# Value products one pair later, padded new values and reordered loads in a paged attention kernel on one core

## The chip, the core and the metric

The kernel runs on one core of a Trainium2 chip. The metric is device time in microseconds (us) from one launch, all of it, constants and layouts of the host excluded. Engines are called as the profile calls them: PE is the matrix engine (PEld its weight loads), DVE the vector engine, ACT the scalar engine, POOL the general-purpose engine, SP the one that here only issues DMAs (SPq, ACTq: issues by SP and ACT).

## The reference

Two residual layers on `x`, shape (32, 32, 512), float32. The first is grouped-query attention (32 query heads, 8 key heads, 128 wide) with a paged cache: each batch row has 16 pages of 32 keys, named by its row of a block table, and 32 new keys and values of its own.

```python
q = _rope(_rmsnorm(x @ Wq.T, q_norm_w), pos)           # 32 heads
k = _rope(_rmsnorm(x @ Wk.T, k_norm_w), pos)           # 8 heads
v = x @ Wv.T
k_all = concat([k_cache[block_table], k], axis=1)      # 512 cached + 32 new keys per row
v_all = concat([v_cache[block_table], v], axis=1)
scores = q @ k_all.T * SCALE                            # cached keys past cache_seqlens masked
o = softmax(scores) @ v_all
x = x + o @ Wo.T
x = x + (x @ W.T + 2 * lora(x, top-2 gates))           # second layer
```

## The kernel before

The 1024 rows of x are eight **tiles** of 128 rows; a tile is four batch rows (`ROWS`) of 32 positions. The eight key heads are four **groups** of two (`GK`). The main loop runs groups outside and tiles inside, 32 **steps** `i = g * TILES + t`. Within a step the work is eight **pairs** `p` (batch row `p // 2`, key head `p % 2`); a pair has 128 query rows (4 query heads of the group by 32 positions) against 544 keys. Every engine has its own instruction list, written by hand in a function `body(g, t, final)`; they meet only at semaphores, and each engine runs its list strictly in order. Steps t = 1 to 5 are one loop body, the others are written out.

Products that need more than one pass split both factors in a rounded half (`_hi`) and a rest (`_lo`), and multiply three times (`three_pass`, L193). Per pair:

- PE `score` (L193, to SX), three passes over 17 key slots; the scores of pair p + 2 are made while pair p is worked on.
- DVE `minimum` (L992) adds the mask and finds the extreme value; ACT `exponent` (L776); DVE `normalise` (L997, L999).
- PE `turn_probs` (L537, L538) transposes the probabilities to PT in five matmuls; ACT `take_pT` (L772) copies them to pT; PE `weigh` (L550, L554) multiplies them with the values into O, transposed: four full products with cached values `v_rows` (each two instructions in the trace) and one with the new values `v_new`. The new values of the four batch rows lie in one tile, 32 partitions each, so this last product uses 32 of the array's 128 rows: `v_new[rows, cols]` against `pT[rows, L:L + P]`.
- DVE `take_o` (L1008, L1010) splits O into oT_hi and oT_lo.

In the PE list, pair p is `turn_probs(p)`, `score(p + 2)`, some projections of the next step, `weigh(p)`. After the last pair come the 24 products of `project_out` (to MISC), which DVE adds to y (`add_y`, L1027). The add of L1027 ends a step in the tables below.

In the same step the next step's q, k, v are projected (`proj`, to PROJ, three blocks of 12 products), taken by ACT (`take_block`), squared by ACT, and rotated: DVE `rotate` (L975, L979), then POOL `make_rstd` (L1258, L1261) and `rotate_sum` (L1269, L1278); PE `turn_k` and `turn_q` transpose the result.

POOL also issues the gathers of cached values (`gather`, L1225, four indirect DMAs for each batch row), makes the rotation table (`make_table`), and copies the new values (`keep_v`, L1286). SP fetches the keys: 12 pages of each batch row, 48 a step (L267), ACT the other 4; the page's byte offset is read from the list `pages` into a register (`read_pages`). SP also loads x, the mask, weights (`next_half`), the running y, and the cached keys of the next group, which PE, ACT and DVE turn and split in eight **units** (`turn_unit`) and SP stores back to DRAM as `kT_pages` (`store_unit`). Before a group's first step all eight stores must have landed (`ku_stored`); ACT and SP wait for this in step t = 7.

## Time and profile before

| | |
|---|---|
| median of 3 runs | 1611.72 us (1608.89 to 1619.95) |
| the profiled execution, its own time | 1600.16 us |
| its span, first to last instruction | 1598.3 us |
| PE busy | 1379.9 us, 86% |
| POOL busy | 948.5 us, 59% |
| DVE busy, ACT busy | 823.5 us, 662.0 us |
| mean granted clock of PE | 0.923 |
| HBM traffic | 188 GB/s over the span |

The busy time of an engine leaves out register reads, semaphores and the issue of DMAs by SP and ACT, so SP has none at all and must be read from its timeline. PE's busy time counts the modelled end of a matmul, which overlaps the next one's start. Step ends, by the end of L1027's adds, are at 139.0 (step 0), 354.3 (step 5), 510.7 (step 8), 1521.5 (step 30) and 1551.7 us (step 31). Steps with t = 6, 7 and 0, around the change of a group, also carry the weight loads; they are called boundary steps below (nine of them between step 6 and step 24), and the other 21 of steps 1 to 30 plain steps.

### The profile page before, as it was taken

Reading aid. Unit: us, or ns where it says so; the run is one execution under the profiler, and the core shown is the slowest. Engines: PE = TensorE matmul, PEld = TensorE weight load, DVE = VectorE, ACT = ScalarE, POOL = GpSimd, SP = SyncE. Lnnn points to the kernel's source line nnn. Section 1 sums busy time; section 2 is a strip of 40 time slices with the busy share of each in tenths; the row PEclk is TensorE's granted clock in tenths of the full one; section 3 lists DMA queues with packets and bytes.
Section 4 is the critical chain, followed back from the end, with each engine's and each line's share of the span. In section 5 each row is a group of like instructions: output and inputs, shape, how many; then the busy total and the mean of one; then the engine's idle time right before and its main releaser. Section 6 shows DMA issues by size and latency. Waiting matters only on the chain.

```text
span 1598.3 us, 33745 instructions
## 1 busy us (share of the span) xinstructions
PE 1379.9 (86%) x8000; PEld 1171.2 (73%) x8000; DVE 823.5 (52%) x2193; ACT 662.0 (41%) x1742; POOL 948.5 (59%) x1270
## 2 busy tenths in 40 slices
PE   4369999998788999999887999999878989888899
PEld 3258787777676777778676787877767877777777
DVE  5445455455455445555545555545545454545544
ACT  3243444444343344444344444444434344434431
POOL 4446666665565667666555666666655666666500
PEclk9588999898999899999898999999879899989999
DMA  8675766678656676677667666667666565656721
GB/s 293 194 211 156 202 193 199 187 202 246 181 177 182 174 201 190 189 200 212 195 178 212 191 199 197 187 191 222 203 197 183 149 182 165 176 168 174 211 77 53
DMA packets 393726, 299.69 MB, mean 187 GB/s; under 512 B 45905, under 2 KB 349297, under 8 KB 393458
## 3 DMA queue, kind: packets, MB, share of 16 engines
q1 hardware_dynamic: 292386, 193.37, 41.3%
q0 software_dynamic: 24576, 67.14, 14.5%
q10 hardware_dynamic: 76656, 37.98, 8.3%
q8 instruction: 38, 0.62, 0.2%
q14 instruction: 70, 0.57, 0.1%
HBM read 271.27 MB, written 29.13 MB: 188 GB/s over the span
## 4 chain that ended last, share of the span: by engine, by line
PE 42%; issue 16%; SPq 15%; DVE 9%; ACT 4%; DMA 4%; another core or an unknown queue 4%; ACTq 3%; POOL 1%; DVEq 0%; POOLq 0%
PE MISC L193 11%; PE O L550 8%; SPq L267 8%; PE SX L193 6%; PE PROJ L193 5%; PE O L554 4%; PE PT L537 4%; DVE soft L992 2%; ACTq L267 2%; ACT pT L772 2%; DMA stage<-in_wqkv 2%; SPq L319 2%; DVE rope_v L979 2%; SPq L266 1%
## 5 line engine op out<-in xcount | busy, mean ns | idle before, releaser
L1225 POOL DMA_INDIRECT v_rows<-in_kv,step_idx x512 | 506.6, 990 | 195.6 <-issue 132.8
L550 PE MATMUL O<-pT,v_rows 128*128 128x128 f32 x2048 | 304.3, 295 | 132.1 <-ACT pT L772 124.6
L776 ACT ACTIVATE soft<-soft,min_all 128x544 f32<-128x544 f32 x256 | 191.7, 749 | 524.0 <-DVE min_all L992 373.3
L550 PEld LDWEIGHTS O<-pT,v_rows 128*128 128x128 f32 x2048 | 276.2, 205 | 173.8 <-ACT pT L772 154.6
L1008 DVE CAST oT_hi<-O 128x128 fp32r<-128x128 f32 x256 | 73.8, 288 | 409.1 <-PE O L554 303.8
L772 ACT ACTIVATE pT<-PT 128x640 f32<-128x640 f32 x256 | 179.7, 702 | 177.6 <-PE PT L538 103.8
L193 PE MATMUL SX<-kT,qT_hi 128*128 128x288 f32 (+1 forms) x1024 | 242.5, 327 | 8.0 <-DVE qT_lo L1021 3.9
L992 DVE CUSTOM_DVE_ANT_0 soft<-SX,mask 128x544 f32<-128x544 f32 x256 | 184.4, 720 | 52.2 <-PE SX L193 23.8
L193 PEld LDWEIGHTS SX<-kT,qT_hi 128*128 128x128 f32 x1024 | 170.7, 202 | 17.8 <-issue 6.7
L537 PE MATMUL PT<-ident,soft 128*128 128x128 f32 x1024 | 180.7, 303 | 2.1 <-issue 2.1
L999 DVE TENSOR_SCALAR soft<-soft,rden 128x544 f32<-128x544 f32 x256 | 157.4, 615 | 9.1
L193 PE MATMUL PROJ<-w_hi,x_hi 128*128 128x512 f32 x384 | 152.5, 397 | 7.8 <-ACT raw L739 4.8
L1269 POOL TENSOR_TENSOR rope_u<-rope_u,rope_v 128x512 f32<-128x512 f32 (+1 forms) x96 | 109.2, 1138 | 80.6 <-DVE rope_v L979 80.6
L193 PE MATMUL SX<-kT,qT_lo 128*128 128x288 f32 (+1 forms) x512 | 155.1, 303 | 0.0
L193 PE MATMUL PROJ<-w_hi,x_lo 128*128 128x512 f32 x384 | 151.9, 396 | 0.0
L193 PE MATMUL PROJ<-w_lo,x_hi 128*128 128x512 f32 x384 | 151.7, 395 | 0.0
L537 PEld LDWEIGHTS PT<-ident,soft 128*128 128x128 f32 x1024 | 123.3, 152 | 32.2 <-issue 6.6
L554 PE MATMUL O<-pT,v_new 32*128 32x128 f32 x512 | 132.2, 340 | 0.0
L1258 POOL TENSOR_SCALAR meansq<-sumsq 128x4 f32<-128x4 f32 (+1 forms) x96 | 23.1, 240 | 158.9 <-ACT squares L746 128.6
L193 PE MATMUL MISC<-wo_hi,oT_hi 128*128 128x512 f32 x256 | 113.0, 441 | 3.7 <-DVE oT_lo L1010 3.6
L193 PE MATMUL MISC<-wo_lo,oT_hi 128*128 128x512 f32 x256 | 105.1, 411 | 0.0
L554 PEld LDWEIGHTS O<-pT,v_new 32*128 32x128 f32 x512 | 80.4, 196 | 33.5 <-issue 5.8
(205 smaller groups left out, 2170.0 us busy)
## 6 DMA issues: line engine op xcount, KB each, us to landing
kT<-kT_pages SPq DMA_DIRECT2D x1536, 64.0 KB
kT<-kT_pages ACTq DMA_DIRECT2D x512, 64.0 KB
mask<-mask_rows SPq DMA_DIRECT2D x64, 272.0 KB
kT_pages<-k_split SPq DMA_DIRECT2D x24, 512.0 KB
stage<-in_wqkv SPq DMA_DIRECT2D x22, 512.0 KB
x_raw<-in_xT SPq DMA_DIRECT2D x32, 256.0 KB
stage<-in_wo SPq DMA_DIRECT2D x16, 512.0 KB
v_rows<-in_kv,step_idx POOLq DMA_INDIRECT x512
```

What stands on the lines that cost most here:

```text
L193: mm = nc.tensor.matmul(out_ps, a, b, start=(c == 0 and k == 0), stop=(c == stop_at and k == 2))
L267: eng.dma_start(kT[:, b, j, :, :, :].rearrange("p z h s -> p (z h s)").bitcast(U8), kT_bytes[bass.ds(at, PAGE_BYTES)].rearrange("(d n) -> ...
L537: nc.tensor.transpose(PT[:, c * P:(c + 1) * P], probs[:, p % 2, c * P:(c + 1) * P], ident[:, :])
L550: nc.tensor.matmul(O[:, 0:P], v_rows[:, b, c, h * D:(h + 1) * D], pT[:, c * P:(c + 1) * P], start=c == 0, stop=False)
L554: nc.tensor.matmul(O[:, 0:P], v_new[rows, cols], pT[rows, L:L + P], start=False, stop=True).then_inc(sm["pv_done"], 1)
L772: nc.scalar.activation(pT[:, :], PT[:, 0:L + P], ACT.Copy).then_inc(sm["pT_ready"], 1)
L776: nc.scalar.activation(probs[:, p % 2, 0:KEYS], scores[:, p % 2, :], ACT.Exp, bias=min_all[:, p:p + 1], scale=-1.0, accum_out=den[:, p:p + ...
L992: V.tensor_tensor_reduce(scores[:, p % 2, :], SX[:, SX_AT[p % 2]:SX_AT[p % 2] + KEYS], mask[:, b, :], 1.0, BIG, ALU.add, ALU.min, min_all[ ...
L999: V.tensor_scalar(probs[:, p % 2, 0:KEYS], probs[:, p % 2, 0:KEYS], rden[:, p:p + 1], None, ALU.mult).then_inc(sm["probs_ready"], 1)
L1008: V.tensor_copy(hi, src).then_inc(sm["o_hi_ready"], 1)
L1225: G.indirect_dma_start(v_rows[:, b, c, :], None, v_half[:, :], bass.IndirectOffsetOnAxis(ap=step_idx[:, b * LC + c:b * LC + c + 1], axis=0 ...
L1269: G.tensor_tensor(rope_u[:, 0:w], rope_u[:, 0:w], rope_v[:, 0:w], ALU.add).then_inc(sm["sum_ready"], 1)
```

## The change

1. **PE order.** `weigh(p)` moves behind `turn_probs(p + 1)` and `score(p + 3)` of the following pair; pT gets two buffers. Over a step's end `turn_probs` of the next step's pair 0 and `score` of its pair 2 go ahead of `project_out`, which is split in three parts with `weigh` of pair 7 after the first. ACT and DVE lists follow.
2. **New values.** POOL writes, in place of the copy `v_new` (128 x 256), the tile `v_own` (128 x 4 x 256): for each of the four batch rows all 128 partitions, zero outside its own 32. The last product of `weigh` then uses all 128 rows.
3. **Order of loads.** A key unit is turned at pair 6 of the step before it is due (unit u in step u - 1; unit 0 at pair 2 of step 0), where it was at pair 1 of step u - 1 and pairs 2 and 3 of step 0. The weight halves move in HI_AT and LO_AT, and SP issues them at other places; half 5 is now the first load after the unit's store in t = 7. SP waits for the stored y after two batch rows of pages, not before the first. POOL makes the table of step i + 2 near the end of step i, where it made the table of i + 1 at the start.
4. **Page lists.** The byte offsets of all 32 steps are made at the start, four groups at once, and stored in DRAM (`page_bytes`); a step loads its own 64 (`load_list`), and registers are read at fixed addresses.
5. **Start.** SP issues the first key loads ahead of x and the weights, PE turns all eight units first, the split units are staged in wo_hi and wo_lo, ACT no longer waits for the page stores before block 2, and the halves that POOL split are split by DVE.
6. To make room: q_rot shares rope_v's memory (DVE's `rotate` then waits for `q_turned`), `squares` has two slots, the sign of the sine moves from a table into DVE's `scalar_tensor_tensor`, and the key turn goes to PROJ.

The core of the diff:

```diff
-        squares = sb("squares", [P, 512], BF16)
+        squares = sb("squares", [P, 2, D], BF16)
         sumsq = sb("sumsq", [P, NBLK, REP])
         meansq = sb("meansq", [P, REP])
         rstd = sb("rstd", [P, REP])
-        q_rot = sb("q_rot", [P, 512])
+        q_rot = rope_v
         k_rot = sb("k_rot", [P, GK * D])
         v_next = sb("v_next", [P, GK * D])
-        v_new = sb("v_new", [P, GK * D])
+        v_own = sb("v_own", [P, ROWS, GK * D])
...
+        HI_AT = ((6, 1), (6, 2), (6, 4), (6, 6), (7, 0), (7, 2), (0, 0), (0, 1), (0, 4), (0, 5))
+        LO_AT = ((6, 2), (6, 3), (6, 5), (6, 7), (7, 1), (7, 3), (0, 1), (0, 2), (0, 5), (0, 6))
+        L1_HI_AT = ((6, 1), (6, 2), (6, 5), (6, 6))
+        L1_LO_AT = ((6, 2), (6, 3), (6, 6), (6, 7))
         WO_FIRST = 2 * NBLK
...
-            if t == 0:
-                return {2: 0, 3: 1}.get(p)
-            return t + 1 if t < TILES - 1 and p == 1 else None
+                return t + 1 if p == 6 else None
+            if t == 0 and p == 2:
+                return 0
+            return t + 1 if t < TILES - 1 and p == 6 else None
 
         def next_tile(g, t):
...
+            def load_list(i):
+
+                sp.dma_start(pages[:, :], page_dram[bass.ds(i, 1), :]).then_inc(sm["pages_in"], 16)
+
...
-                    next_half(g + 1, 0)
-                    next_half(g + 1, 1)
-                if final and fixed and t == TILES - 2:
-                    for m in range(2):
-                        sp.wait_ge(sm["w_lo_ready"], GROUPS * HALVES + m - 1)
-                        sp.dma_start(stage[:, m, :, :], w1T.rearrange("p (c n) -> p c n", c=KC)[:, 2 * m:2 * m + 2, :]
-                                     ).then_inc(sm["stage1_in" if m else "stage0_in"], 16)
+                if not final:
+                    if fixed and t == 0:
+                        load_kn(n_unit, g + 1, 0)
+                    else:
+                        store_unit(n_unit + t, g + 1, t, False)
+                        if not fixed or t < TILES - 1:
+                            load_kn(n_unit + t + 1, g + 1, t + 1)
+                if fixed and t == TILES - 1 and not final:
+                    next_half(g + 1, 5)
+                if not last:
+                    read_pages(i + 1, 0)
+                    if fixed and t == TILES - 1:
+                        sp.wait_ge(sm["ku_stored"], (g + 2) * 16 * UNITS)
+                    load_pages(i + 1, 0)
+                if not (final and fixed and t >= TILES - 2):
+                    load_x(i + 2, (t + 2) % TILES if fixed else t + 2)
+                if not last:
+                    load_pages(i + 1, 1)
                 sp.wait_ge(sm["y_stored"], (i + 1) * 16)
...
+                if not (isinstance(i, int) and i * PAIRS + p == 0):
+                    pe.wait_ge(sm["pT_ready"], i * PAIRS + p)
                 for c in range(LC):
                     nc.tensor.transpose(PT[:, c * P:(c + 1) * P], probs[:, p % 2, c * P:(c + 1) * P], ident[:, :])
                 nc.tensor.transpose(PT[:, L:L + P], probs[:, p % 2, new_rows(b)], ident[:, :]
...
+                cols = slice(h * D, (h + 1) * D)
                 for c in range(LC):
-                    nc.tensor.matmul(O[:, 0:P], v_rows[:, b, c, h * D:(h + 1) * D], pT[:, c * P:(c + 1) * P],
+                    nc.tensor.matmul(O[:, 0:P], v_rows[:, b, c, cols], pT[:, p % 2, c * P:(c + 1) * P],
                                      start=c == 0, stop=False)
-                cols = slice(h * D, (h + 1) * D)
-                rows = slice(b * SEQ, (b + 1) * SEQ)
-                nc.tensor.matmul(O[:, 0:P], v_new[rows, cols], pT[rows, L:L + P], start=False, stop=True
+                nc.tensor.matmul(O[:, 0:P], v_own[:, b, cols], pT[:, p % 2, L:L + P], start=False, stop=True
                                  ).then_inc(sm["pv_done"], 1)
 
-            def project_out(i, h, wcount):
-                if h == 0:
+            def project_out(i, h, part, wcount):
+                first, n = part
+                if h == 0 and first == 0:
                     pe.wait_ge(sm["y_added"], CREDIT + i)
                 pe.wait_ge(sm["w_lo_ready"], wcount + 2 * h)
                 pe.wait_ge(sm["o_ready"], CREDIT + i * PAIRS + PAIRS - GK + h + 1)
                 mm = three_pass(MISC[:, :], lambda c: (oT_hi[:, c, :], oT_lo[:, c, :]),
-                                lambda c: (wo_hi[:, c, :], wo_lo[:, c, :]), REP, h * REP, GQ - 1)
-                if h == GK - 1:
+                                lambda c: (wo_hi[:, c, :], wo_lo[:, c, :]), n, h * REP + first, GQ - 1)
+                if h == GK - 1 and first + n == REP:
                     mm.then_inc(sm["y_done"], 1)
 
...
+                    if p > 0:
+                        turn_probs(i, p)
                         score(i, p + 2)
                     for k, c in fill[p] if not last else []:
                         proj(i + 1, k, (c, 1), wcount)
-                    u = unit_at(t, p)
-                    if u is not None and not final:
-                        n = UNITS + g * UNITS + u
-                        pe.wait_ge(sm["kn_in"], (n + 1 - UNITS) * 16)
-                        pe.wait_ge(sm["y_added"], CREDIT + i)
-                        pe.wait_ge(sm["ku_ready"], n)
-                        turn_unit(MISC, kn)
+                    unit(p)
                     if not last and p == 4:
                         pe.wait_ge(sm["y_added"], CREDIT + i)
-                        if not final:
-
-                            if fixed:
-                                pe.wait_ge(sm["ku_ready"], UNITS + g * UNITS + min(t + 2, UNITS))
...
-                                pe.wait_ge(sm["ku_ready"], UNITS + g * UNITS + t + 2)
+                        if not final and fixed and t == 0:
+                            pe.wait_ge(sm["ku_ready"], UNITS + g * UNITS + 1)
                         turn_q(i + 1, 0)
                     if not last and p == 5:
...
+                    if p > 0:
+                        weigh(i, p - 1)
+                p = PAIRS - 2
+                turn_probs(i, p)
+                if not last:
+                    score(i + 1, 0)
+                    turn_q(i + 1, 1)
+                unit(p)
+                weigh(i, p - 1)
                 turn_probs(i, PAIRS - 1)
                 if not last:
-                    pe.wait_ge(sm["kT_new_ready"], i + 2)
-                project_out(i, 0, g * HALVES + WO_FIRST + 2)
+                    score(i + 1, 1)
+                weigh(i, p)
+                if not last:
+                    turn_probs(i + 1, 0)
+                    score(i + 1, 2)
+                u = unit_at(t, p)
+                if u is not None and not final:
+                    pe.wait_ge(sm["ku_ready"], UNITS + g * UNITS + u + 1)
+                project_out(i, 0, (0, REP // 2), g * HALVES + WO_FIRST + 2)
                 weigh(i, PAIRS - 1)
-                if not last:
-                    score(i + 1, 1)
-                project_out(i, 1, g * HALVES + WO_FIRST + 2)
+                project_out(i, 0, (REP // 2, REP // 2), g * HALVES + WO_FIRST + 2)
+                project_out(i, 1, (0, REP), g * HALVES + WO_FIRST + 2)
 
             walk(pe, body)
...
-                hi, lo = half_parts(m)
-                pool.wait_ge(sm["w_hi_ready"], m + 1)
-                pool.wait_ge(sm["w_lo_ready"], m)
-                G.tensor_tensor(lo, w1_stage[:, 2 * (m % 2):2 * (m % 2) + 2, :], hi.bitcast(F32), ALU.subtract
-                                ).then_inc(sm["w_lo_ready"], 1)
+                shape = [P, ROWS, GK * D]
+                G.tensor_tensor(v_own[:, :, :], v_next[:, :].rearrange("p (a n) -> p a n", a=1).to_broadcast(shape),
+                                row_mask[:, :].rearrange("p (b a) -> p b a", a=1).to_broadcast(shape), ALU.mult
+                                ).then_inc(sm["v_own_ready"], 1)
...
                 tn = 0 if fixed and t == TILES - 1 else t + 1
                 keep_v(i)
-                if not last:
...
+                def next_values(b):
+                    pool.wait_ge(sm["pv_done"], CREDIT + i * PAIRS + b * GK + GK)
+                    pool.nop(nofuse=True)
+                    gather(b, 0, LC)
+
+                for k in range(2):
                     make_rstd(i + 1, k)
                     rotate_sum(i + 1, k)
-                    if k == 0:
-                        for row in range(ROWS - 1):
-                            pool.wait_ge(v_in[row], (i + 1) * 16 * LC)
-                        take_indices(tn, 0, ROWS - 1, 2 * i + 3)
-                    pool.wait_ge(sm["pv_done"], CREDIT + i * PAIRS + k * GK + GK)
-                    pool.nop(nofuse=True)
-                    gather(k, 0, LC)
...
+                    make_table(i + 2, (t + 2) % TILES if fixed else t + 2)
+                next_values(1)
+                next_values(2)
 
             walk(pool, body)
 
```

POOL's list, plain steps, first part: names are output<-inputs; `v_next` holds the projected new values. Before:

```order
L1286 COPY v_new<-v_next 128x256
L1238 ISA
L1244 TENSOR_TENSOR table<-cos,norm_w 128x64
L1246 TENSOR_TENSOR table<-sin,mask_w 128x64
L1244 TENSOR_TENSOR table<-cos,norm_w 128x64
```

Now, from the same place to the k rotation:

```order
L1370 TENSOR_TENSOR v_own<-v_next,row_mask 128x1024
L1315 ISA
L1315 COPY step_idx<-v_base 128x4
L1317 ISA
L1308 DMA v_rows<-in_kv,step_idx 128x256 x4
L1337 ISA
L1338 REGISTER_ALU
L1340 TENSOR_SCALAR meansq<-sumsq 128x2
L1343 TENSOR_TENSOR rstd<-meansq,minus_half 128x2
L1351 TENSOR_TENSOR rope_u<-rope_u,rope_v 128x256
L1360 TENSOR_TENSOR k_rot<-rope_u,rstd 128x256
```

The copy has become an operation of four times the elements, and the table's eight operations are gone from here; they follow after the last rotation.

PE's list at the end of a plain step: PT is where probabilities are turned, SX the scores, O the value product, MISC the output projection. Before, behind `weigh(6)` and `score` of the next step's pair 0:

```order
L624 REGISTER_ALU
L509 MATMUL PROJ<-ident,q_rot 128x128 x4
L537 MATMUL PT<-ident,soft 128x128 x4
L538 MATMUL PT<-ident,soft 128x128
L560 REGISTER_ALU
L193 MATMUL MISC<-wo_hi,oT_hi 128x512
L193 MATMUL MISC<-wo_lo,oT_hi 128x512
L193 MATMUL MISC<-wo_hi,oT_lo 128x512
```

Now, from `weigh(6)`:

```order
L591 MATMUL O<-pT,v_rows 128x128 x4
L593 MATMUL O<-pT,v_own 128x128
L577 MATMUL PT<-ident,soft 128x128 x4
L578 MATMUL PT<-ident,soft 128x128
L194 MATMUL SX<-kT,qT_hi 128x288 x2
L194 MATMUL SX<-kT,qT_lo 128x288
L565 REGISTER_ALU
L194 MATMUL SX<-kT,qT_hi 128x256 x2
L194 MATMUL SX<-kT,qT_lo 128x256
L679 REGISTER_ALU
L600 REGISTER_ALU
L194 MATMUL MISC<-wo_hi,oT_hi 128x512
```

The turn (L577) and the score behind it belong to the next step's pairs 0 and 2; before, both stood behind all 24 products of the projection.

SP's list from step t = 6 to t = 7: kT is the tile of fetched keys, kT_pages the key pages in DRAM. Before:

```order
L464 DMA y_running<-y_tile 128x512
L400 REGISTER_ALU
L402 DMA y_tile<-y_running 128x512
L406 ISA
L319 TENSOR_LOAD pages
L323 ISA
L267 DMA kT<-kT_pages 128x512 x12
```

Now:

```order
L500 DMA y_running<-y_tile 128x512
L372 REGISTER_ALU
L375 ISA
L375 DMA kT_pages<-k_split 128x8x128
L318 REGISTER_ALU
L313 ISA
L313 DMA stage<-in_wqkv 128x1024
L343 REGISTER_ALU
L345 TENSOR_LOAD pages
L442 ISA
L350 ISA
L278 DMA kT<-kT_pages 128x512 x12
```

The store of the group's last unit (L375) and a weight half (L313) now stand between the store of y and the first page; L442 is the wait for all eight stores.

## Rows read from the trace of the kernel before

**Rows 1.** Page, part 1: engine, busy us, share of the span, instructions.

```profile
PE 1379.9 (86%) x8000; PEld 1171.2 (73%) x8000; DVE 823.5 (52%) x2193; ACT 662.0 (41%) x1742; POOL 948.5 (59%) x1270
```

**Rows 2.** Windows at step ends: stretch, length, busy by engine, PEclk, DMA share, GB/s.

```profile
0.00:139.00 139.00, 74.45 (x344) 61.35 (x345) 66.86 (x157) 44.90 (x111) 65.40 (x102) 0.78 0.72 218
139.00:354.30 215.30, 199.39 (x1212) 169.77 (x1211) 114.93 (x321) 95.48 (x261) 145.06 (x196) 0.97 0.69 195
354.30:510.70 156.40, 129.19 (x728) 109.09 (x728) 80.69 (x205) 65.98 (x167) 91.13 (x119) 0.90 0.68 199
510.70:1521.50 1010.80, 906.02 (x5294) 771.46 (x5294) 527.55 (x1426) 435.87 (x1161) 645.60 (x855) 0.93 0.65 189
1521.50:1551.70 30.20, 28.31 (x182) 23.50 (x181) 13.71 (x43) 10.74 (x21) 1.29 (x2) 1.00 0.29 92
1551.70:1598.30 46.60, 42.53 (x250) 36.08 (x248) 19.77 (x48) 8.99 (x25) 0.00 (x0) 1.00 0.12 46
```

**Rows 3.** Waits: engine, line, whom it waited for: us in total, times, longest.

```profile
PE O L550 <- ACT pT L772: 124.6, 86, 7.6
PE MISC L509 <- DVE kT L1014: 13.3, 1, 13.3
PE MISC L509 <- DVE k_split L958: 11.4, 3, 5.3
ACT k_split L768 <- DMA kT_pages<-k_split: 25.3, 3, 10.9
```

**Rows 4.** Timeline of PE, one pair: start us, us, engine, line, operation [idle before].

```profile
700.02 0.27 PE L538 MATMUL PT<-ident,soft 128*128 128x128 f32 x1
...
702.26 1.06 PE L550 MATMUL O<-pT,v_rows 128*128 128x128 f32 x8
...
703.25 0.48 PE L554 MATMUL O<-pT,v_new 32*128 32x128 f32 x2
...
703.66 0.66 PE L537 MATMUL PT<-ident,soft 128*128 128x128 f32 x4
```

**Rows 5.** Timeline of PE in step 7, a boundary step.

```profile
424.13 2.08 PE L550 MATMUL O<-pT,v_rows 128*128 128x128 f32 x8 [7.59 <-ACT pT L772]
```

**Rows 6.** Timeline of POOL, one round of step 18.

```profile
931.59 1.02 POOL L1225 DMA_INDIRECT v_rows<-in_kv,step_idx  x1 [0.78 <-POOL step_idx L1232]
...
937.43 0.19 POOL L1258 TENSOR_SCALAR meansq<-sumsq 128x2 f32<-128x2 f32 x1 [1.07 <-ACT squares L746]
...
939.54 0.72 POOL L1269 TENSOR_TENSOR rope_u<-rope_u,rope_v 128x256 f32<-128x256 f32 x1 [0.85 <-DVE rope_v L979]
...
947.76 0.19 POOL L1258 TENSOR_SCALAR meansq<-sumsq 128x4 f32<-128x4 f32 x1 [0.69 <-issue]
...
950.39 1.28 POOL L1269 TENSOR_TENSOR rope_u<-rope_u,rope_v 128x512 f32<-128x512 f32 x1 [1.31 <-DVE rope_v L979]
...
969.44 0.39 POOL L1286 COPY v_new<-v_next 128x256 f32<-128x256 f32 x1 [1.90 <-PE O L554]
...
973.65 1.02 POOL L1225 DMA_INDIRECT v_rows<-in_kv,step_idx  x1 [0.80 <-POOL step_idx L1232]
```

**Rows 7.** Groups of instructions, POOL: count, busy us, mean ns of one.

```profile
L1293 POOL TENSOR_TENSOR w_lo<-soft,w_hi 128x1024 fp32r<-128x1024 f32 x2 | 4.8, 2381 | 0.2
```

**Rows 8.** Timeline of SP over the same step: DMA issues.

```profile
931.95 0.36 SPq L464 DMA_DIRECT2D y_running<-y_tile  x1
...
937.25 5.38 SPq L267 DMA_DIRECT2D kT<-kT_pages  x12
...
957.26 14.44 SPq L267 DMA_DIRECT2D kT<-kT_pages  x24
972.03 0.33 SPq L333 DMA_DIRECT2D mask<-mask_rows  x1
974.01 0.36 SPq L464 DMA_DIRECT2D y_running<-y_tile  x1
```

**Rows 9.** Timeline of ACT in step 0.

```profile
47.76 0.60 ACT L739 ACTIVATE raw<-PROJ 128x512 f32<-128x512 f32 x1 [14.12 <-issue]
```

447 lines of the change are left out of this document (242 added, 205 removed).

## The prediction

> **What bounds the kernel now.** I read the shares first, then the stretches between step ends, then PE's waits, and then one plain step on each engine whose list is strictly in order. PE is busy for 1379.9 of 1598.3 us, POOL for 948.5, DVE and ACT for about half or less [rows 1]. Over the 30 full steps (139.0 to 1521.5 us) PE is busy for 199.39 + 129.19 + 906.02 = 1234.6 of 1382.5 us [rows 2]: the kernel is paced by PE, with 148 us of idle time inside. A plain step takes 215.3 / 5 = 43.1 us, a boundary step 156.4 / 3 = 52.1 us [rows 2]; 21 of the one and 9 of the other give 1374, against the 1382.5 there are. Of PE's idle time, 124.6 us in 86 pieces ends when ACT has copied the turned probabilities to pT, which `weigh` needs [rows 3]. The granted clock is 0.97 in the first plain stretch and 0.90 in the first boundary stretch [rows 2]; 1.0 stands for the level of 2.4 GHz and 0.5 for 1.2, so some time of each goes at the lower one.
>
> The reader should then leave PE. In one plain step POOL's list goes from one gather of row 3 to the next in 973.65 - 931.59 = 42.06 us, and what it waits for there is short: 1.07, 0.85, 1.31 and 1.90 us [rows 6]. An idle 0.69 us with no releaser also stands behind a group of gathers [rows 6], so of the 1.07 and the 1.90 about 0.7 each is no wait. Real waits are 0.4 + 0.85 + 1.31 + 1.2 = 3.8 us, and POOL's round needs **38.3 us**. That is more than its busy time tells (645.60 us over 22 steps is 29.3 a step [rows 2]), since the 0.3 us between indirect DMAs and the waits for its own indices are not busy. SP is as close: from one store of y to the next it takes 42.06 us, and between the mask's issue (over at 972.36) and the store it waits 1.65 us [rows 8]; **up to 40.4 us** is its own issuing, with 24 pages in 14.44 us at one place and 12 in 5.38 at another, so a part of it can shrink. Three in-order lists lie within 3 us of each other.
>
> **The change, part by part.** The sum is made against the profiled execution, 1600.16 us for a span of 1598.3 (1.9 outside), which is 0.7% under the median of 1611.72.
>
> *The last value product on all 128 rows.* In the pair shown, eight full instructions of `weigh` start at 702.26 and end 1.06 us later; one alone lasts 0.27 [rows 4], so starts are (1.06 - 0.27) / 7 = 0.113 us apart. The two on 32 rows begin at 703.25, 0.20 us after the last full start by that spacing, and PE's next work begins at 703.66, 0.41 later, where two full ones would take 0.23 [rows 4]. The whole takes 1.40 us against 10 x 0.113 = 1.13: **0.27 us a pair, 2.2 a step, 69 over 256 pairs** of PE time. The end of a group of full products is taken from the start of the next; whether the turn behind it can then start as early is not shown, so the bounds are 0 and 0.27, and I take 0.27.
>
> A rule speaks against this term. The Trainium skill (TensorE: Matmul & The Clock Gate, "Part 3: Packing small matmuls") says that a product with 32 rows takes the same time as one with 128, and that a weight load overlaps running matmuls only where the row groups differ. By that, the 32-row product would cost nothing extra, this term would be 0, PE's own plain step 39.9 + 0.6 = 40.5 where I get 38.3 below, and the sum about 20 us longer by the boundary steps; the row shows 0.41 us for what takes 0.23 on full rows, so the trace disagrees.
>
> *Products one pair behind.* `weigh(p)` now has the turn and the score of the next pair ahead of it, 1.4 us of PE work by rows like those of [rows 4], and pT is double, so ACT's copy is out of the way: most of the 124.6 us [rows 3] goes. That is 3 us of a plain step. In a boundary step it is more: one wait in step 7 is 7.59 us [rows 5], where ACT stands at a weight half that SP issues late; the half is now issued at the head of the step. O stays single, and `weigh` still waits for DVE's split of the pair before, which has a whole pair's time. ACT and DVE, at 41 and 52%, cover their moved jobs; were they late by more than the pair's 5 us, `turn_probs` would wait instead.
>
> By PE alone a plain step would be: busy 199.39 / 5 = 39.9 us at clock 0.97 [rows 2], less 2.2, is 37.7, with 0.6 for what waits remain 38.3.
>
> *POOL's new product.* The copy of 0.39 us [rows 6] becomes 128 x 1024 elements with two inputs. The nearest row is POOL's own subtraction of that size, 2.38 us [rows 7]; the copy times four is 1.56, and twice the 1.28 us of 128 x 512 [rows 6] is 2.56. So +1.2 to +2.2, taken +2.0. The table's eight operations are only moved. POOL's round becomes 38.3 + 2.0 = **40.3 us**, above PE's 37.7. POOL takes the bound: PE finds the rotated q of block 2 late at `turn_q` of head 1, just after pair 6's turn and the next step's first score, because POOL must sum and scale block 1 only after ACT's squares of it, then gather row 0, then do block 2. The hoisted turn and score behind that point wait with it. I put a plain step at **40.6**, 0.3 over POOL's round for a hand-over that is not perfect. The padding's gain of 2.2 us on PE is thus mostly not seen, since the engine that pays for it becomes the slow one.
>
> *SP.* It gains one small load of a list a step, at the 0.33 to 0.36 us of its other issues [rows 8], and a wait for ACT's register read, which comes at the head of ACT's step and is long over. It loses the wait for the stored y, which is now covered by pages and was part of the 4.9 us between y's issue and the first page (932.31 to 937.25 [rows 8]). Reading registers at fixed addresses changes nothing that the rows show. Its round was at most 40.4; with one thing added and one gone I put it near 40, just under POOL's.
>
> *Key units and stores.* PE's waits of 11.4 us at the q turn for a unit's split [rows 3] go. A new wait comes: unit 7 is turned at pair 6 of step t = 6 and stored by SP only after y is stored at that step's end, while ACT at the head of t = 7 waits for all eight stores before it reads its registers. Its copies and evictions queue behind that wait, and PE's projection of block 1 waits for ACT to take block 0. Rows for a landing: ACT waited 25.3 us in 3 for such a store, 10.9 the longest [rows 3]. From the last value product to that point PE has 30 of the 242 matmuls of a step (1212 / 5 [rows 2]), the widest ones: 5 us by their number, and I take 8 for their width. By the same count y is added after 5 and the store issued at about 6, to land 5 to 10 later: 3 to 8 us of new wait, three times. SP's pages stand behind the same landing.
>
> So for the boundary steps: 52.1, less about 3.7 a step for the extra pT waits (three times the 7.59, and ACT's other late copies), less 1.3 for the unit's split, less the 2.5 that a plain step gains, and 5 / 3 = 1.7 more for the new wait, 42.9; the lower clock there (0.90) lets PE be the bound for part of it. I take **44**.
>
> *Start and end.* PE waits 13.3 us at the first q turn [rows 3], behind ACT, which idles 14.12 us for the page stores before block 2 [rows 9]; both go, but 4 MB of stores and then the pages must still come first, at the 218 GB/s that step 0 moves already [rows 2], and POOL has still 12 gathers before `keep_v`. Of 139.0 us I take 9 off, bounds 0 and 20. Step 31 has no projection and no gathers but one: 30.2 less 2.2 and 0.5 is 27.5. The tail's 46.6 us [rows 2] is untouched.
>
> **Sum:** 130 + 21 x 40.6 + 9 x 44 + 27.5 + 46.6 = 1452.7, and 1.9 outside the span: 1455 for an execution like the profiled one. The median may lie up to 0.7% above; I say **1458**.
>
> **Rivals.** *PE stays the bound (25%).* POOL's idle 0.7 us behind gathers could be overlapped or its operations run at 1.2 us extra; then plain steps are 38.3, boundary steps 41.5, the start 128: 128 + 804 + 374 + 27 + 46.6 + 1.9 = 1382. For it: POOL's 38.3 rests on one step. Against it: that step's round closes to 0.1 us.
>
> *The hand-overs add (20%).* SP near 40, POOL at 40.3 and PE at 37.7 wait for each other in turn, POOL's elementwise work slows down beside a denser DVE, and the new wait at t = 7 comes at its upper end. Plain steps 42.3, boundary steps 47.5, start 136: 136 + 888 + 428 + 28 + 46.6 + 1.9 = 1529.
>
> *The pT wait only changes its name (6%).* If normalised probabilities come late, the turn waits where the product did. Only the padding's gain is left, 69 us less what POOL takes: about 1560. Against it: the scores are still two pairs ahead, and no row of PE's waits names the normalising step.
>
> *Slower than before (2%).* POOL's round is the mechanism, at `keep_v`: it paces every step, and 30 steps average 1382.5 / 30 = 46.1 us, so from a round of 46.5 on, that is a product of 8.6 us instead of 2.4, the kernel is slower. At 10 us the round is 47.9 and the time 130 + 30 x 47.9 + 74 + 2 = 1643. Only a POOL held up by another engine for most of that product would bring this; by [rows 7] it would have to take over three times the row nearest to it.
>
> The likeliest, POOL's round, has 47%. The range must hold 8 in 10: from 1375 (the PE case, nearly whole) to 1530 (the hand-over case up to its middle). About 1% is what can be told from no change; faster by over 1% has 96%, within 1% 2%, slower 2%.
>
> **What would show it.** The product with new values should start 0.11 us behind the full ones, and PE's waits for pT fall under 20 us. POOL's product should last 2.1 to 2.6 us, POOL should wait for others by less than 2 us in a plain step, and PE's longest waits should name POOL's last rotation at `turn_q` of head 1. At t = 7 ACT should stand 5 to 10 us for the stores. The prediction is wrong where POOL still waits 3 us or more a step: then either PE bounds (no PE idle, about 38 us a step) or SP does (no wait ahead of its y store).

## The result

In the comparison that the forecast was made for, the change takes 1692.26 us (median of 4 runs, 1676.94 to 1701.28) against 1610.31 us before (4 runs, 1600.05 to 1619.95): a ratio of 1.050, 95% interval 1.040 to 1.060. It is 5% slower, where 1458 us and 9% faster were forecast.

That is half of the result. Later comparisons, each of kernels on one chip, fell on five chips. On four the kernel before took 1518 to 1527 us, and on the three of them where the changed kernel itself ran it took 1457 to 1462 us (ratio 0.956, interval 0.950 to 0.963, for the best measured). On the fifth the kernel before took 1610.5 us again. The sign of this change depends on something that a chip has or has not, and it can be read in a trace. I call the first kind quiet and the other kind holding. The record does not name the chip of the first comparison; by the time of the kernel before, and by its traces, it is of the holding kind.

Means over step ends (DVE's add to y, as in the table ahead of the prediction), profiled executions, us:

| kernel, chip | start | plain step (21) | boundary step (9) | step 31 | whole |
|---|---|---|---|---|---|
| before, holding | 139.0 | 43.8 | 51.4 | 30.3 | 1600.2 |
| forecast | 130 | 40.6 | 44 | 27.5 | 1455 |
| change, holding | 129.0 | 49.0 | 51.4 | 24.4 | 1692.7 |
| change, quiet | 118.4 | 40.0 | 47.9 | 24.1 | 1461.2 |
| padding alone (experiment 4), quiet | 131.7 | 39.4 | 47.5 | 27.8 | 1461.6 |

From quiet to holding the change loses 21 x 9.0 + 9 x 3.5 + 10.6 = 231 us, all of the difference. Against the kernel before on a holding chip its plain steps are 5.2 us longer (109 us over 21), the start 10 and step 31 6 us shorter: the 93 us by which it is slower.

**The profile after.** Busy times, first of the change in the first comparison, then of the same kernel on a quiet chip; they answer to [rows 1]:

```profile
span 1690.9 us, 34346 instructions
PE 1312.7 (78%) x8000; PEld 1160.1 (69%) x8000; DVE 872.7 (52%) x2195; ACT 664.6 (39%) x1741; POOL 985.9 (58%) x1264
```

```profile
span 1459.4 us, 34346 instructions
PE 1250.8 (86%) x8000; PEld 1119.2 (77%) x8000; DVE 861.2 (59%) x2195; ACT 656.8 (45%) x1741; POOL 984.1 (67%) x1264
```

PE has lost 67 us of busy time against [rows 1] even on the first chip, so the padding does its part; POOL's work is the same on both. The mean granted clock is 0.896 in the one and 0.942 in the other (0.923 before), so the slower one stands more of its time at the lower level, 1.2 GHz; its PE is busy 62 us longer with the same 8000 matmuls. Now the waits of the first (engine and line, what it waited for, us in total, times, longest us), against [rows 3]:

```profile
ACT pT L827 <- remote: 138.1, 43, 7.4
DVE soft L1060 <- remote: 135.1, 51, 7.4
DVE oT_hi L1076 <- remote: 102.3, 28, 7.0
ACT kT L808 <- remote: 23.9, 22, 2.0
POOL v_own L1370 <- remote: 10.7, 6, 1.9
PE MISC L194 <- DVE oT_lo L1078: 101.7, 25, 7.1
PE MISC L194 <- issue: 42.7, 15, 5.7
PE O L591 <- ACT pT L827: 3.5, 4, 1.1
```

The waits of `weigh` for pT are gone (124.6 us before). In their place stand 144 us at MISC, ahead of `project_out`. And ACT, DVE and POOL together wait 410 us for "remote": a signal that came when no instruction that gives it had just ended, and no transfer had landed. There is one core and no other one in the program. The kernel before has these rows too, from the same view as [rows 3]:

```profile
DVE oT_hi L1008 <- remote: 59.9, 22, 4.2
ACT pT L772 <- remote: 41.7, 34, 2.8
ACT raw L735 <- remote: 6.1, 1, 6.1
ACT kT L753 <- remote: 3.9, 8, 0.5
DVE soft L992 <- remote: 1.4, 5, 0.6
```

113 us in all, and I had not read them. In the change's trace on a quiet chip there is no such row. What PE and POOL wait for there is this:

```profile
POOL meansq L1340 <- ACT squares L799: 152.9, 39, 8.2
PE PROJ L547 <- POOL rope_v L1360: 49.1, 25, 4.9
PE O L591 <- ACT pT L827: 23.7, 23, 1.3
```

The difference is told by the page's chain of work that ended last (the shares by engine), holding, then quiet:

```profile
PE 32%; issue 18%; SPq 14%; DVE 10%; another core or an unknown queue 9%; POOL 7%; DMA 4%; ACT 3%; ACTq 2%; DVEq 0%; POOLq 0%
```

```profile
PE 40%; POOL 22%; issue 14%; SPq 7%; DMA 5%; DVE 5%; ACT 4%; ACTq 3%; POOLq 1%; DVEq 0%
```

What a remote wait is shows in the timeline of a step's end (start us, duration, engine, line; idle time before it in brackets), change, holding chip:

```profile
620.49 0.39 PE L593 MATMUL O<-pT,v_own 128*128 128x128 f32 x2
620.61 9.21 SPq L278 DMA_DIRECT2D kT<-kT_pages  x10
621.03 0.95 POOL L1308 DMA_INDIRECT v_rows<-in_kv,step_idx  x1 [0.30 <-issue]
621.92 0.28 PE L194 MATMUL SX<-kT,qT_lo 128*128 128x256 f32 x1
626.03 0.94 POOL L1308 DMA_INDIRECT v_rows<-in_kv,step_idx  x1 [0.30 <-issue]
628.51 0.29 DVE L1076 CAST oT_hi<-O 128x128 fp32r<-128x128 f32 x1 [6.99 <-remote]
628.57 0.70 ACT L827 ACTIVATE pT<-PT 128x640 f32<-128x640 f32 x1 [6.18 <-remote]
629.27 0.76 PE L194 MATMUL MISC<-wo_hi,oT_hi 128*128 128x512 f32 x1 [7.07 <-DVE oT_lo L1078]
```

PE ends `weigh` of pair 6 at 620.9, the hoisted turn at 621.4 and the hoisted score at 622.2. DVE waits for the first and gets its signal at 628.5; ACT waits for the second and gets its at 628.6. Two pieces of work that ended 0.5 us apart are told within 0.1 us of each other, 7.6 and 7.1 us late. PE then has nothing left to do until DVE has split O. The ends of matmuls are modelled, but their records stop here for 7 us, and inside this pause, at 625.2 us, the granted clock falls from 1.0 to 0.5. In the same time SP issues 10 pages in 9.21 us, 0.92 each. No semaphore stands between them, only two moves of a register for each; in the trace these moves stand too, and SP's records go on in steps of about 0.7 us (621.33, 622.05, 622.76, 623.47, 624.17). Around it POOL issues eight gather DMAs in a row, from 617.14 to 626.97. The same place on the quiet chip:

```profile
570.05 8.99 SPq L278 DMA_DIRECT2D kT<-kT_pages  x18
576.41 0.95 POOL L1308 DMA_INDIRECT v_rows<-in_kv,step_idx  x1 [0.30 <-issue]
577.24 0.39 PE L593 MATMUL O<-pT,v_own 128*128 128x128 f32 x2
577.66 0.29 DVE L1076 CAST oT_hi<-O 128x128 fp32r<-128x128 f32 x1
577.93 0.51 PE L194 MATMUL SX<-kT,qT_hi 128*128 128x288 f32 x2
578.77 0.39 PE L194 MATMUL MISC<-wo_hi,oT_hi 128*128 128x512 f32 x1
```

The same eight gathers in a row (0.95 us each), but DVE has its signal by the modelled end of the product, `project_out` follows the score without a gap, and a page takes 0.50 us.

Is that one place or the rule? In the trace of the kernel before, 61 of its 70 remote waits end within 1.5 us behind the last gather of a run (0.9 us in the median), a stretch that makes up 12% of the span; in the third kernel of experiment 12 it is 60 of 66. In the change on the holding chip 104 of 150 end within 2 us behind a run, and the other 46 inside one. And SP's records follow each other at 0.675 to 0.725 us 273 times in or just behind such runs and 4 times elsewhere; in the change on a quiet chip it is 5 times and 6. So on a holding chip the holds go with the runs of gathers, in the kernel before as well.

The Trainium skill (DMA: Bandwidth & Descriptors, "SWDGE vs HWDGE vs iDMA") says that GpSimd writes its descriptors into rings in SBUF, that DVE can lock it out of that, and that DMAs issued by SP or ACT never touch this path and are immune to that interference. No run here shows that rule at work: the gathers are issued as fast on either chip (0.95 us each at the places shown), and what is late are SP's own issues and PE's signals.

### The profile page after: what moved, and what is told of

The parts are those of the page before. It is cut to its first block, busy times and chain, and to the rows that moved or that the text cites. A ratio compares the mean times of both kernels' runs of the same rounds, so it can differ in the third digit from the quotient of the medians.

```text
span 1690.9 us, 34346 instructions
## 1 busy us (share of the span) xinstructions
PE 1312.7 (78%) x8000; PEld 1160.1 (69%) x8000; DVE 872.7 (52%) x2195; ACT 664.6 (39%) x1741; POOL 985.9 (58%) x1264
## 4 chain that ended last, share of the span: by engine, by line
PE 32%; issue 18%; SPq 14%; DVE 10%; another core or an unknown queue 9%; POOL 7%; DMA 4%; ACT 3%; ACTq 2%; DVEq 0%; POOLq 0%
PE MISC L194 10%; SPq L278 9%; PE PROJ L194 5%; PE SX L194 5%; PE O L591 5%; DVE soft L1060 3%; POOL rope_u L1351 2%; PE PT L577 2%; POOL rstd L1343 2%; DVE soft L1067 2%; SPq L345 2%; DMA stage<-in_wo 1%; POOL v_rows L1308 1%; POOL rope_v L1360 1%
## 5 line engine op out<-in xcount | busy, mean ns | idle before, releaser
L591 PEld LDWEIGHTS O<-pT,v_rows 128*128 128x128 f32 x2048 | 286.9, 211 | 60.7 <-issue 41.5
L194 PE MATMUL SX<-kT,qT_hi 128*128 128x288 f32 (+1 forms) x1024 | 236.0, 319 | 89.0 <-DVE kT L1082 51.1
L194 PE MATMUL MISC<-wo_hi,oT_hi 128*128 128x512 f32 x256 | 124.6, 487 | 144.4 <-DVE oT_lo L1078 101.7
L194 PEld LDWEIGHTS SX<-kT,qT_hi 128*128 128x128 f32 x1024 | 164.5, 196 | 100.8 <-issue 98.5
L577 PE MATMUL PT<-ident,soft 128*128 128x128 f32 x1024 | 160.8, 281 | 46.6 <-ACT pT L827 28.7
L1067 DVE TENSOR_SCALAR soft<-soft,rden 128x544 f32<-128x544 f32 x256 | 181.5, 709 | 9.1
L194 PEld LDWEIGHTS MISC<-wo_hi,oT_hi 128*128 128x128 f32 x256 | 57.7, 225 | 165.6 <-issue 155.2
L577 PEld LDWEIGHTS PT<-ident,soft 128*128 128x128 f32 x1024 | 124.7, 146 | 56.9 <-issue 38.4
L1370 POOL TENSOR_TENSOR v_own<-v_next,row_mask 128x1024 f32<-128x1024 f32 x32 | 60.5, 1892 | 128.7 <-PE O L593 107.0
L1042 DVE TENSOR_TENSOR rope_u<-raw,table 128x512 f32<-128x512 f32 (+1 forms) x96 | 57.9, 603 | 146.6 <-ACT raw L789 79.4
L785 ACT ACTIVATE raw<-PROJ 128x256 f32<-128x256 f32 x32 | 12.3, 386 | 305.3 <-PE PROJ L194 232.8
```

The costliest lines, as they stand in the source:

```text
L194: mm = nc.tensor.matmul(out_ps, a, b, start=(c == 0 and k == 0), stop=(c == stop_at and k == 2))
L577: nc.tensor.transpose(PT[:, c * P:(c + 1) * P], probs[:, p % 2, c * P:(c + 1) * P], ident[:, :])
L591: nc.tensor.matmul(O[:, 0:P], v_rows[:, b, c, cols], pT[:, p % 2, c * P:(c + 1) * P], start=c == 0, stop=False)
L1042: V.tensor_tensor(rope_u[:, 0:w].rearrange("p (r d) -> p r d", d=D), raw[:, 0:w].rearrange("p (r d) -> p r d", d=D), table[:, tc:tc + 1, : ...
L1067: V.tensor_scalar(probs[:, p % 2, 0:KEYS], probs[:, p % 2, 0:KEYS], rden[:, p:p + 1], None, ALU.mult).then_inc(sm["probs_ready"], 1)
L1370: G.tensor_tensor(v_own[:, :, :], v_next[:, :].rearrange("p (a n) -> p a n", a=1).to_broadcast(shape), row_mask[:, :].rearrange("p (b a) - ...
```

## The experiments

Two theories. **A**: while POOL issues a long run of gathers, signals of other engines are held back; the change makes that run eight long and lays it over the step's end. **B**: the new order itself is at fault, since the hoisted score wants keys that come late. POOL's list in the change ends a step with block 2's rotation, the table, `next_values(1)` and `next_values(2)`; the second may start only behind `weigh` of pair 5, which now comes one pair later, so the two meet. Before, the rotation of block 2 stood between these two gathers.

**1. One gather ahead of the table.**

```diff
+                next_values(1)
                 if not (final and fixed and t == TILES - 2):
                     make_table(i + 2, (t + 2) % TILES if fixed else t + 2)
-                next_values(1)
                 next_values(2)
```

> The changed kernel with one swap in POOL's list: the gather of batch row 1 goes ahead of make_table, so that eight indirect loads in a row become two runs of four with the table (about 2.5 us) between them. Theory A (a long run of POOL's indirect loads holds back the semaphore signals of the other engines, and the run of eight lies over the step's end): the 5 to 7 us wait ahead of project_out in plain steps falls below 3 us, 3 to 4 us a plain step, about 1610 to 1630 us. Rival B (the new order of PE's list or the keys' loads are the cause): nothing that B rests on moves, 1692 us within 10.

1460.5 us, ratio 0.959 (0.950 to 0.968), far below both, but beside a kernel before of 1524 us. There was no remote wait in it. So this said nothing on A; it said that the chip mattered.

**2. Direct loads for gathers**, in the change, then (10) in the kernel before.

```diff
-                    G.indirect_dma_start(v_rows[:, b, c, :], None, v_half[:, :],
...
+                    G.dma_start(v_rows[:, b, c, :], kv[(b * LC + c) * P:(b * LC + c + 1) * P, GK * D:2 * GK * D]).then_inc(v_in[b], 16)
```

> The changed kernel with every indirect gather of cached values replaced by a direct load of the same size (128 rows of 1 KB) from fixed rows, issued by POOL at the same place; the values read are so not those that the block table names. Theory A: no run of indirect loads, so signals are not held, the wait ahead of project_out falls below 2 us and SP issues a page in 0.5 us throughout; 1480 to 1560 us. Rival B (bytes and DMA engines are short, or the order on PE): as many bytes and the same order, so 1650 us or more.

1398.3 us, ratio 0.916 (0.909 to 0.924). Again, on another chip:

> The changed kernel with direct loads in place of gathers again (values of fixed rows). Where before takes 1525 us, 1398 us as before. Where signals are held: under 1450 us if the gathers are what holds them, over 1600 us if something else on the chip does.

1395.8 us, on a quiet chip again. The values are wrong and the rows fixed, but the bytes and PE's order are the change's, so neither of these sets its 40.0 us there. What fell is POOL: 747.3 us busy and not 984.1, and the plain step is 37.1 us. That a direct load also lands in another way than a gather was not separated.

**3. Eight gathers in a row in the kernel before** (row 1's behind row 2's).

```diff
-                    gather(k, 0, LC)
+                    if k != 1:
+                        gather(k, 0, LC)
+                    if k == 2:
+                        gather(1, 0, LC)
```

> The kernel before with the gather of row 1 moved behind that of row 2, so that eight indirect loads follow each other at the step's end; row 1's values are wanted only at pair 2 of the next step. Theory A: signals held over the step's end, 2 to 5 us a plain step more, 1660 to 1730 us. Rival B: POOL's list has slack and the values are not wanted yet, so within 1% of 1610 us.

1514.7 us, ratio 0.993 (0.989 to 0.998). The trace has 31 runs of eight, and on a quiet chip they cost nothing, as B said. A speaks of the other kind and is untouched.

**4. The padding alone**, in the kernel before.

```diff
-                nc.tensor.matmul(O[:, 0:P], v_new[rows, cols], pT[rows, L:L + P], start=False, stop=True
+                nc.tensor.matmul(O[:, 0:P], v_own[:, b, cols], pT[:, L:L + P], start=False, stop=True
```

> The kernel before with the padded new values alone (part 2, with the memory and the sign of part 6 that make room for it; order of the lists as before). The prediction's own term: 0.27 us a pair, 2.2 us a step, 69 us off PE, if PE's products are what a pair waits for: 1540 us. Rival (the pair is set by the hand-over of probabilities through ACT and by held signals): PE gets 66 us of busy time back and waits as much longer for pT, 1590 to 1615 us.

1462.4 us, ratio 0.960 (0.953 to 0.968): 62 us less, against 69 forecast for this term. POOL's new product, the shared memory of q_rot and the sign of part 6 are in it, the order of the lists is not. It is as fast as the whole change on a quiet chip. It never ran on a holding one.

**5. The change itself again.**

> The changed kernel as it is, run beside the others. The first four runs were made on a chip where the kernel before took 1524 us and not 1610 us, and there no issue of SP was held up during a run of gathers (22 us in all, against 254 us in the first trace of before). If the loss belongs to held signals, which a chip may have or not, then where before takes 1524 us the change takes 1450 to 1480 us (ratio 0.95 to 0.97), and where before takes 1610 us it takes 1690 us again. If the loss belongs to the change's own order, the ratio is 1.05 on either.

1459.5 us, ratio 0.956 (0.950 to 0.963). Two more chips were tried:

> The changed kernel again, to see whether another chip holds signals. If before takes about 1524 us here, the change takes 1455 to 1465 us; if before takes about 1610 us, the change takes about 1690 us and its trace has waits put down to no releaser of the program (remote) of over 200 us.

> The changed kernel again, on whichever chip this is. If before takes about 1525 us, the change takes 1455 to 1465 us; if before takes about 1610 us, the change takes about 1690 us.

1461.7 us (0.959, 0.950 to 0.968) and 1457.1 us (0.960, 0.953 to 0.966), both quiet.

**6. Without the hoist over the step's end.**

```diff
                 weigh(i, p)
-                if not last:
-                    turn_probs(i + 1, 0)
-                    score(i + 1, 2)
...
                 project_out(i, 1, (0, REP), g * HALVES + WO_FIRST + 2)
+                if not last:
+                    turn_probs(i + 1, 0)
+                    score(i + 1, 2)
```

> The changed kernel with turn_probs of the next step's pair 0 and score of its pair 2 moved back behind project_out, on PE and DVE. Rival B (the score needs keys that come late, and holds project_out up): at least as fast as the change, by up to 5 us a step where signals are held. Theory A: the wait ahead of project_out is the held signal of weigh(6), which this order has as well; where signals are not held it is 0.5 to 2 us a step slower than the change, since the gap at project_out now has no work in it: +15 to +60 us.

1507.3 us, ratio 0.989 (0.985 to 0.992), 48 us more than the change: the plain step is 42.4. B falls on a quiet chip: the hoist gains 2.4 us a plain step there. On a holding chip it was not tried alone, but the second kernel of experiment 12 keeps the hoist there and is faster than the kernel before.

**7. Block 2's rotation ahead of all gathers.**

```diff
-                next_values(0)
                 make_rstd(i + 1, 2)
                 rotate_sum(i + 1, 2)
+                next_values(0)
+                next_values(1)
...
-                next_values(1)
                 next_values(2)
```

> The changed kernel with another order in POOL's list: block 2's rotation ahead of the gather of row 0, then the gathers of rows 0 and 1, the table, the gather of row 2. In the trace with the gather of row 1 ahead of the table PE waits 1.8 us a plain step for block 2's rotation, which stood behind the gather of row 0. If POOL's order is what bounds a plain step there: 1.5 to 2.5 us less than that kernel, ratio to before 0.93 to 0.94. If PE's own work bounds it: 0.955 to 0.96 as there.

1485.4 us, ratio 0.974 (0.967 to 0.981): a miss, 26 us more than the change. PE's 49.1 us of waits for POOL's rotation went, and this came (waits of this kernel):

```profile
PE PROJ L194 <- ACT v_next L787: 93.2, 30, 5.7
ACT v_next L787 <- POOL v_own L1370: 85.8, 25, 4.4
```

`v_own`, behind the last gather, is late, ACT may not overwrite v_next before it, and PE waits for ACT. The wait was moved, not removed.

**8. v_own on DVE.**

```diff
-                keep_v(i)
+                pool.wait_ge(sm["pv_done"], CREDIT + i * PAIRS)
...
                 add_y(i, y_all[:, TILES - 1, :] if last else y_tile[:, :])
+                if not last:
+                    keep_v(i + 1)
```

> The changed kernel with the product v_own on DVE, behind the add to y at the step's end, and no longer on POOL (32 times 1.9 us there). If POOL's round bounds a plain step where signals are not held: 1 to 1.9 us a step less, 1400 to 1430 us there. If PE or the chain of pairs bounds it: DVE's 1.1 to 1.3 us lie in the way of the next step's minimum, 1460 us or up to 1% more.

1455.3 us, ratio 0.956 (0.949 to 0.963), a miss: 1400 to 1430 was expected. Against the change on the same chip (1461.7) POOL's busy time fell by 51 us and the time by 6, which is not told from nothing. PE still waited 50.6 us for POOL's rotation, and POOL's waits for ACT's squares grew from 152.8 to 186.7 us: most of what its list was spared it spent waiting.

**9. The last product on 32 rows again**, in the change.

```diff
-                nc.tensor.matmul(O[:, 0:P], v_own[:, b, cols], pT[:, p % 2, L:L + P], start=False, stop=True
+                nc.tensor.matmul(O[:, 0:P], v_own[rows, b, cols], pT[rows, p % 2, L:L + P], start=False, stop=True
```

> The changed kernel with the last product of weigh on the 32 rows of the batch row again (the zero rows are written by POOL and not used). If POOL's round bounds a plain step: PE gets back its 0.27 us a pair, 2.2 us a step, and the time grows by less than that, 0 to 1 us a step, up to 1490 us. If PE's work does: 2.2 us a step, 1530 us, all that padding gave.

1491.2 us, ratio 0.978 (0.971 to 0.986). Against the change on the same chip PE's busy time rises by 70 us, the time by 30, a plain step by 1.2 us of the 2.2: with the lists of the change about half of what padding gives is hidden.

**10. Direct loads in the kernel before.**

> The kernel before with every indirect gather replaced by a direct load of the same size from fixed rows, so that the values are not those of the block table. Where signals are held during gathers: 1610 us falls to 1500 us or less. Where they are not: POOL's list gets shorter, but PE waits for pT and not for POOL, so 1490 to 1524 us.

1537.8 us, ratio 1.008 (1.004 to 1.011): POOL's list is no bound there, and its relief gives nothing. It is even 14 us slower, above the 1490 to 1524 us expected; why is not shown. The first half of the expectation met no holding chip.

**11. ACT's wait for the key stores moved** behind block 0's copies in step t = 7, alone and with 8.

```diff
-                    if isinstance(t, int) and t == TILES - 1:
-                        act.wait_ge(sm["ku_stored"], (g + 2) * 16 * UNITS)
...
                         square_block(i + 1, p // 2)
                     jobs(p)
+                    if late and not last:
+                        act.wait_ge(sm["ku_stored"], (g + 2) * 16 * UNITS)
+                        act.nop(nofuse=True)
+                        next_pages(p)
```

> The changed kernel with ACT's wait for the eight key stores (ku_stored, step t = 7) moved from the start of its step to behind block 0's copies, so that PE's projections of block 1 need not wait for it. In the change's trace on a chip without held signals PE stands 5.3 to 6.3 us before L194's projections in each of three steps t = 7 (ACT v_next). If this wait is on the path: 10 to 17 us less, 1443 to 1450 us. If the keys' loads, which then start later, take its place: within 3 us of 1460.

> The late wait and v_own on DVE together. Additive: 4 us less than the late wait alone, about 1440 us. If nothing of it is on the path: 1455 us.

1435.8 us, ratio 0.946 (0.942 to 0.950), and with v_own on DVE 1437.0 (0.947): the late wait alone is the fastest kernel here that computes the reference, 21 us under the change beside it (1457.1), where 10 to 17 were expected. With v_own on DVE another 4 us were expected and did not come. In a quiet trace of the change and in this kernel's the same wait reads:

```profile
PE PROJ L194 <- ACT v_next L787: 18.3, 5, 6.3
```

```profile
PE PROJ L194 <- ACT v_next L787: 1.3, 2, 0.8
```

**12. A hold put in by hand.** These fell on the holding chip. DVE's `take_o` of pair 6 waits for POOL's last gather of the step; once in the change, once in the order of experiment 1, once in the kernel before.

```diff
                 next_values(2)
+                pool.nop(nofuse=True)
+                pool.sem_inc(sm["gathers_out"], 1)
...
+                if not last:
+                    dve.wait_ge(sm["gathers_out"], i + 1)
+                    dve.nop(nofuse=True)
                 take_o(i, p)
```

> The changed kernel with a hold put in by hand, to price what the first chip's trace shows: DVE's take_o of pair 6 waits until POOL has issued its last gather of the step (new semaphore gathers_out). In the first trace this signal came 0.9 to 1.4 us behind the run of eight gathers. Theory A (in the change the hand-over at the step's end lies inside that run): 3 to 6 us a step more on a chip without held signals, 1550 to 1650 us. If DVE and PE have slack there: within 1% of 1460 us.

1687.7 us, ratio 1.046 (1.042 to 1.050), beside before at 1610.5. The expectation was made for a quiet chip, and there it was never tried. The change without it took 1692 us in the first comparison, and the plain step is 48.9 us and not 49.0. If that was a chip like this one, the wait put in costs nothing here: the true hold is already as long as the run of gathers.

> The same hold in the kernel whose gather of row 1 stands ahead of the table. The last gather then ends some 2 to 5 us earlier, so at least 2 us a step less than the change with the hold. If the order of the gathers is no matter: the same as that one.

**1554.0 us, ratio 0.964 (0.961 to 0.967).** It differs from the one above by the place of one call, and is 134 us faster; on a quiet chip that place was worth nothing (1460.5 and 1459.5).

> The same hold in the kernel before, whose four runs of gathers stand apart. Theory A: its last gather of the step is issued ahead of or beside pair 6, 0 to 2 us a step, 1525 to 1590 us, so that the change with the hold is slower than before with it. If before suffers as much as the change, the place of the gathers does not explain why one chip turns the sign.

1621.3 us, ratio 1.002 (0.998 to 1.007): the kernel before does not suffer from the wait, and with it the change is slower than before, as A said.

The waits of the kernel with both gathers behind the table, then of the one with the earlier gather:

```profile
ACT pT L827 <- remote: 150.8, 48, 7.5
DVE soft L1060 <- remote: 123.8, 53, 7.4
DVE oT_hi L1076 <- remote: 104.5, 24, 7.0
PE MISC L194 <- DVE oT_lo L1078: 102.8, 24, 7.1
PE MISC L194 <- issue: 39.5, 16, 5.7
```

```profile
ACT pT L827 <- remote: 86.3, 42, 3.8
DVE oT_hi L1076 <- remote: 76.9, 29, 4.2
DVE soft L1060 <- remote: 70.0, 39, 2.3
PE MISC L194 <- DVE oT_lo L1078: 25.5, 21, 4.1
PE MISC L194 <- issue: 5.7, 6, 2.0
```

The longest hold falls from 7.5 to 4.2 us, and PE's wait at `project_out` from 142 to 31 us. A plain step falls from 48.9 to 43.7. The wait put in by hand also ends earlier in the second kernel; but if it cost nothing in the first, it is the true hold that became shorter.

**What stays open.** Why one chip holds signals and others do not; whether the gathers cause it, or only meet it: experiment 2 never ran on a holding chip, and neither did the order of experiment 1 without the wait. "Held signals" may be only the visible side, since SP's register moves, which signal nobody, stand too. It may be the engines' lists that are slowed, or the recording of them: every execution on record has a recorded span and clock, so none shows whether the recording takes part. Shown is that the holds go with the runs of gathers and that the time follows the place of the gathers there.

## Why the prediction was wrong

- **The step that failed.** "I put a plain step at **40.6**, 0.3 over POOL's round for a hand-over that is not perfect." In the comparison a plain step is 49.0 us, 176 us more over 21, and a boundary step 51.4 for 44, 67 us more over nine; that is all of the miss (1692.7 for 1455). The hand-over from `weigh` over DVE to `project_out`, for which the sum has no term, took 144 us of PE's time, and late signals 410 us over all engines. Nothing in the sum stands for held signals, and none of the four rivals has them; the slower one asked for a product of 8.6 us on POOL, and it is 1.89. The rows that show the hold (113 us of "remote", 6.1 us the longest) stood in the view of [rows 3], and I did not ask what they were. What a change does with such a stretch is to be asked as of any wait: before, it was four runs of four gathers a step, with a rotation between any two, and the table behind the fourth. The new list puts the gathers of rows 1 and 2 behind both, in one run of eight, where nothing covers the hand-over. The prediction's "The table's eight operations are only moved" looks at what they take, and not at what they part.
- **Padding, 69 us.** Right in size: 62 us by itself on a quiet chip (experiment 4). A product with new values starts 0.11 us behind the one before it (620.38 and 620.49), as forecast. The Trainium skill (TensorE: Matmul & The Clock Gate, "Why this matters for your kernels", and not Part 3, where the prediction places it) says that a single product with 32 rows takes the same time as one with 128. By that it should have given nothing; experiments 4 and 9 (62 and 30 us) disagree for a product that stands between full ones.
- **One pair behind.** The waits for pT went: 3.5 us left on the first chip, 23.7 us on a quiet one, where 20 was the limit named. But on a quiet chip the whole change is no faster than padding alone (1459.5 and 1462.4 us, on two chips). Its gain of 13 us at the start and 4 in step 31 is there, but plain steps are 0.6 us longer than with padding alone, and boundary steps 0.4. That the new order gains nothing because POOL's part of each step has become the slow one fits the waits, but no run has the new order without the rest.
- **POOL's round as the bound.** On a quiet chip right in size (40.0 us for 40.6) and half right in kind. PE's longest regular wait names POOL's last rotation (49.1 us in 25), and taking POOL's gather work away gives 37.1 us, for 37.7 of PE's work and 38.3 with its waits. But POOL waits for others 3.4 us in a plain step, nearly all of it for ACT's squares, where under 2 was forecast and 3 named as the sign of being wrong; so its round needs 36.6 us, not 40.3. The 38.3 for the round before rested on one step: counted in the same way over all 21 plain steps of that trace, POOL waited 5.7 us a step for the others, not 3.8. The product of `keep_v` took 1.89 us, for 2.4 (2.0 over the copy's 0.39). Neither PE alone nor SP, which waited 224 us for y, is the bound in its place. The waits point to a chain that goes through ACT's squares, POOL's last rotation and PE; experiment 8, which spares POOL work ahead of that wait, fits it, but no run shows the chain by itself.
- **New wait at t = 7, 3 to 8 us, three times.** Right: 5.5 to 6.3 us, and 21 us gained by removing it.
- **Boundary steps, 44.** Too low by 3.9 on a quiet chip, 35 us over nine. More than half of it is a slip in the sum: 52.1 - 3.7 - 1.3 - 2.5 + 1.7 is 46.3 and not 42.9, since the new wait was taken off where it is to be added. For the rest, waits of the turn for ACT's copy, up to 6.5 us, came in place of the pT waits.
- **Start, 130.** 129.0, and 118.4 on a quiet chip. Step 31: 24.4 for 27.5.

That the quiet chips' 1457 to 1462 us lie on the forecast of 1458 is luck. The forecast took 152 us off a kernel before of 1610 us; on a quiet chip that kernel takes 1524 us, and the change gains 64. So the forecast left in the 86 us that a holding chip costs the kernel before, and took off 88 us too much for the change; the two cancel. Within the sum, +35 at the boundaries stands against -12 at the start, -13 in plain steps and -3 in step 31.

## What to carry to other kernels

Read the waits that name nothing of the program ("remote", "another core or an unknown queue") before any other, lay them beside the runs of indirect loads, and keep such a run short and away from the one hand-over that nothing covers; a few small jobs between two gathers are a break that should be kept. Where a change makes one engine the slow one, gains made on the others do not add to it. And a ratio from one chip is a fact about that chip: look whether the kernel before takes the same time there as in its own profile.

## What the runs showed of the hardware

- The kernel before took 1610 us on one chip and 1518 to 1527 us on four others, and kernels with gathers had the same busy time for them on either kind (990 to 1021 ns each). The 15 traces from the four, of the change and of variants of both kernels, have no remote wait.
- On a holding chip signals of PE reached DVE and ACT up to 7.6 us after the modelled end of the products, several at once, and SP's page issues took 0.92 us and not 0.50 in the same stretch. In the kernel before 61 of 70 such waits ended within 1.5 us behind a run of gathers.
- A direct load issued by POOL costs its list less than a gather of the same 128 KB: POOL's busy time fell from 984 to 747 us with 512 of them exchanged, 0.46 us each.
